# Row maxima of a unit turned by one transpose of 16 columns instead of four of 4, negated on 16 partitions, and sent as pieces of 128 tokens

## What is computed

```python
for lvl in range(LEVELS):                       # 4 levels
    x = query[:, ::2 ** lvl, :]
    outs.append(_mha(x, in_proj_w[lvl], in_proj_b[lvl], out_w[lvl], out_b[lvl]))
current = outs[-1]
for lvl in range(LEVELS - 2, -1, -1):
    current = _upsample_linear(current, outs[lvl].shape[1]) @ up_w[lvl].T + up_b[lvl] + outs[lvl]
...
h = silu(x @ w1 * s1) * (x @ w2 * s2)           # feed-forward part, widths 256 and 1024
h = gelu(gelu(h @ h1 * s) @ h2 * s);  y = h @ w3 * s3
```

## Time and profile before

| | before |
|---|---|
| median of 3 runs | 3819.87 us (3819.08 to 3824.79) |
| the profiled execution, its own time | 3822.95 us |
| its span in the trace | 3819.7 us |
| mean granted TensorE clock | 0.966 of full speed |
| PE busy | 3545.6 us, 93% |
| ACT busy | 2607.4 us, 68% |
| DVE busy | 2539.7 us, 66% |
| POOL busy | 1134.5 us, 30% |

### The profile page before, as it was taken

How to read it: one execution, slowest core, us unless ns; L and a number is a source line. 1 busy time by engine, 2 the same in 40 slices (tenths; PEclk the granted TensorE clock), 3 DMA queues, 4 the chain that set the end, 5 groups by cost and what they waited for, 6 DMA issues and landing times. The chain is left out here.

```text
span 3819.7 us, 59270 instructions
## 1 busy us (share of the span) xinstructions
PE 3545.6 (93%) x20995; PEld 1428.9 (37%) x20995; DVE 2539.7 (66%) x4805; ACT 2607.4 (68%) x3266; POOL 1134.5 (30%) x1060
## 2 busy tenths in 40 slices
PE   5899999989989999989989998859999999999998
PEld 3333333333333333333333332224444444444444
DVE  4787988988888888897897899833334333334333
ACT  2788788878878878878878888834444444444443
POOL 2243454454364364363354444220000000000000
PEclk6999989999999999999998999979999999999999
DMA  4523333332332342242342233110000000000000
GB/s 145 175 76 92 106 98 93 95 104 83 97 117 82 95 125 76 90 121 79 95 128 74 88 103 106 51 51 11 13 12 13 12 23 12 12 12 15 20 12 12
DMA packets 227902, 269.85 MB, mean 71 GB/s; under 512 B 51268, under 2 KB 187524, under 8 KB 226976
## 3 DMA queue, kind: packets, MB, share of 16 engines
q1 hardware_dynamic: 218352, 257.09, 22.6%
q10 hardware_dynamic: 9216, 8.39, 0.7%
HBM read 159.75 MB, written 101.45 MB: 68 GB/s over the span
## 5 line engine op out<-in xcount | busy, mean ns | idle before, releaser
L957 ACT ACTIVATE a_probs<-a_p_s,a_unit_now 128x1024 f32<-128x1024 f32 x1360 | 1442.4, 1109 | 300.7 <-PE a_p_s L1281 296.3
L1063 DVE TENSOR_REDUCE a_part_max<-a_p_r 128x1 f32<-128x512 f32 x2048 | 1304.1, 676 | 270.1 <-PE a_p_r L1294 265.8
L1294 PE MATMUL a_p_r<-a_k_st,a_q_st 48*128 48x512 f16 (+2 forms) x2944 | 912.2, 380 | 138.0 <-DVE a_part_max L1063 69.6
L1653 PE MATMUL p_h<-f_h_hi,f_w_hi 128*128 128x512 f16 x2048 | 776.3, 379 | 3.0 <-issue 3.0
L1653 PE MATMUL p_h<-f_h_lo,f_w_hi 128*128 128x512 f16 x2048 | 776.2, 379 | 0.0
L1311 PE MATMUL a_p_o<-a_probs,a_v_aug 128*17 128x512 f32 (+2 forms) x5888 | 739.0, 582 | 2.4 <-ACT a_raw L967 2.3
L1281 PE MATMUL a_p_s<-a_q_st,a_k_st 50*128 50x512 f16 (+2 forms) x2944 | 693.6, 374 | 30.7 <-ACT a_probs L957 30.6
L1294 PEld LDWEIGHTS a_p_r<-a_k_st,a_q_st 48*128 48x128 f16 x2944 | 222.7, 94 | 1164.4 <-DVE a_part_max L1063 799.2
L1515 ACT ACTIVATE f_h_f<-p_h,f_sc_now 128x512 f32<-128x512 f32 x256 | 176.0, 688 | 516.3 <-PE p_h L1653 514.3
L1063 DVE TENSOR_REDUCE a_row_max<-a_p_r 128x1 f32<-128x512 f32 (+2 forms) x672 | 426.2, 675 | 82.9 <-PE a_p_r L1294 81.2
L1462 POOL TENSOR_TENSOR f_rstd<-f_var_eps,f_minus_half 128x1 f32<-128x1 f32 x64 | 36.0, 563 | 1240.5 <-DVE f_var_eps L1608 1240.5
(11 more groups left out here) (157 smaller groups left out, 4616.2 us busy)
## 6 DMA issues: line engine op xcount, KB each, us to landing
qk_scratch<-a_qk_room SPq DMA_DIRECT2D x288, 128.0 KB
a_w_lo<-wqkv_inner SPq DMA_DIRECT2D x30, 768.0 KB, 4.5
a_a_lo<-a_attn SPq DMA_DIRECT2D x448, 32.0 KB, 2.0
a_q_st<-qk_scratch SPq DMA_DIRECT2D x64, 192.0 KB, 3.4
a_k_st<-qk_scratch SPq DMA_DIRECT2D x64, 192.0 KB, 4.4
a_o_lo<-wo_inner SPq DMA_DIRECT2D x24, 512.0 KB, 3.5
a_qk_room<-wf SPq DMA_DIRECT2D x23, 512.0 KB, 3.7
a_q_st<-qk_scratch SPq DMA_DIRECT2D x112, 96.0 KB, 2.2
```

Source lines behind the costliest of these rows:

```text
L957: act.activation(probs[:, s % 2, 2 * p:2 * p + 2, :], p_s[:, 2 * p:2 * p + 2, :], ACT.Exp, scale=unit_now[:, lvl:lvl + 1]).then_inc(exp_do ...
L1063: dve.reduce_max(out, src, AX.X).then_inc(max_read.sem, 1)
L1294: ins = pe.matmul(p_a[:, r * size:(r + 1) * size], q_st[rows_of(j, ROWS), query_at:query_at + 128], k_st[rows_of(j, ROWS), key_at:key_at + ...
L1653: ins = pe.matmul(out, a, c, start=first and n == 0, stop=last and n == len(terms) - 1)
```

## The change

`row_max` gets its last two axes swapped, so that the 16 maxima of a query (4 head groups by 4 blocks) lie in the order head, block. One transpose turns all 16 columns at once, into 16 partitions by 128 tokens, where before four transposes turned 4 columns each into 4 partitions by 512. ACT and POOL then work on 16 x 128 instead of 4 x 512. The DMAs send 8 partitions of 128 tokens each (256 bytes) where before they sent 2 of 512 (1024 bytes). So that these pieces form one row, the queries of a fine unit lie in `q_st` one behind the other; for that the "stack" of level 0 loads the queries of each unit of a pair by DMAs of its own: four for `q_st` where there were two, and the same bytes.

```diff
-        row_max = sb("row_max", [128, RING, NQ, HG])
-        neg_f = sb("neg_f", [HG, W])
-        neg_bf = sb("neg_bf", [HG, 2, 2, W], F16)
+        row_max = sb("row_max", [128, RING, HG, NQ])
+        neg_f = sb("neg_f", [HG * NQ, 128])
+        neg_bf = sb("neg_bf", [HG * NQ, 2, 2, 128], F16)
...
+        def query_spot(unit, j):
+
+            return unit.halves[unit.blk] * 2 * W + j % 2 * W
...
+                                    if t == 0 and lvl == 0:
+                                        for blk in range(2):
+                                            part = st[64 * row_half:64 * row_half + ROWS, at + blk * 2 * W:at + (blk + 1) * 2 * W].rearrange("p (h t) -> p h t", h=2)
+                                            sp.dma_start(part, src[:, :, blk * W:(blk + 1) * W]).then_inc(stacked[n].sem, 16)
+                                        continue
                                     sp.dma_start(dst, src).then_inc(stacked[n].sem, 16)
...
-                                    sp.dma_start(placed(q_st, slice(row_at, row_at + 1), UNITS[n], UNITS[n].blk),
-                                                 neg_bf[2 * row_half:2 * row_half + 2, n % 2, i, :]).then_inc(neg_placed[n % 2].sem, 16)
+                                    sp.dma_start(q_st[row_at:row_at + 1, query_spot(UNITS[n], 0):query_spot(UNITS[n], 0) + 2 * W].rearrange("p (r t) -> p r t", t=128),
+                                                 neg_bf[8 * row_half:8 * row_half + 8, n % 2, i, :]).then_inc(neg_placed[n % 2].sem, 16)
...
-                            act.activation(neg_f[:, :], p_a[0:HG, 0:W], ACT.Copy, scale=-1.0 / ONE).then_inc(neg_read.sem, 1)
+                            act.activation(neg_f[:, :], p_a[0:HG * NQ, 0:128], ACT.Copy, scale=-1.0 / ONE).then_inc(neg_read.sem, 1)
...
-                            for q in range(NQ):
-                                ins = pe.transpose(p_a[0:HG, q * 128:(q + 1) * 128], row_max[:, n % RING, q, :], ident[:, :])
-                            ins.then_inc(neg_mm.sem, 1)
+                            pe.transpose(p_a[0:HG * NQ, 0:128], row_max[:, n % RING, :, :].rearrange("p h q -> p (h q)"), ident[:, :])\
+                              .then_inc(neg_mm.sem, 1)
```

More of the change, by code:

```diff
@@ L495, in attention @@
         stored = [sig(f"stored{i}", SLOTS * sum(len(ps) for ps in PROJ[i::2]), 16) for i in range(2)]
-        stacked = [sig(f"stacked{n}", 4, 16) for n in range(len(STACKS))]
+        stacked = [sig(f"stacked{n}", 2 * (1 + len(us)), 16) for n, us in enumerate(STACKS)]
         v_mm, v_done = sig("v_mm", len(V_PAIRS)), sig("v_done", len(V_PAIRS))
@@ L1051, in steps @@
                                 neg_mm.wait(dve, it, u - 2)
-                            slot = row_max[:, u % RING, :, :].rearrange("p q h -> p (q h)")
+                            slot = row_max[:, u % RING, :, :].rearrange("p h q -> p (h q)")
                             q, j, kb, _ = maxima_of(u, m)[0]
                             if lvl == 0:
-                                out = part_max[:, u % RING, q * HG + j, kb:kb + 1]
+                                out = part_max[:, u % RING, j * NQ + q, kb:kb + 1]
                             elif lvl == 3:
-                                out = row_max[:, u % RING, q:q + 2, j:j + 2]
+                                out = row_max[:, u % RING, j:j + 2, q:q + 2].rearrange("p h q -> p q h")
                             else:
-                                out = slot[:, q * HG + j:q * HG + j + parts]
+                                out = row_max[:, u % RING, j:j + parts, q]
                             src = p_a.rearrange("p (r t) -> p r t", r=parts) if parts > 1 else p_a
@@ L1279, in steps @@
                                 for j in (p, p + 2):
-                                    key_at, query_at = spot(unit, half, j) + key, spot(unit, unit.blk, j) + i * size
+                                    key_at, query_at = spot(unit, half, j) + key, query_spot(unit, j) + i * size
                                     ins = pe.matmul(p_s[:, bank_of(j), i * size:(i + 1) * size], k_st[rows_of(j, ROWS + 2), key_at:key_at + 128],
@@ L1289, in steps @@
                             if m == 0 and u == STACKS[STACK_OF[u]][0]:
-                                stacked[STACK_OF[u]].wait(pe, it, 4)
+                                stacked[STACK_OF[u]].wait(pe, it, 2 * (1 + len(STACKS[STACK_OF[u]])))
                             for q, j, kb, r in maxima_of(u, m):
                                 key = q * 128 // size * size if parts > 1 else 0
-                                query_at, key_at = spot(unit, unit.blk, j) + q * 128, spot(unit, kb, j) + key
+                                query_at, key_at = query_spot(unit, j) + q * 128, spot(unit, kb, j) + key
                                 ins = pe.matmul(p_a[:, r * size:(r + 1) * size], q_st[rows_of(j, ROWS), query_at:query_at + 128],
```

## The result

| | before | after |
|---|---|---|
| median of 4 runs | 3820.23 us (3819.08 to 3824.79) | 3796.64 us (3794.89 to 3799.38) |
| span of the profiled execution | 3819.7 us | 3795.0 us |
| mean granted TensorE clock | 0.966 | 0.966 |

The ratio is 0.9937, with a 95% interval of 0.9919 to 0.9954: 23.6 us faster, or 0.6%. The forecast was 3798.

The account below looks back on a forecast made before the run. The attention stage is bound by a chain passing between PE, DVE and ACT, none of them full. PE 12.2, ACT 16.2 and POOL 1.5 sum to 29.9 us, three quarters taken as 22 us: 3798 us, range 3781 to 3813.

Parts of the forecast that it names:

- PE's term: Attention stage: three transposes fewer save 0.33 us a unit, 12.2 us over the 37 units on the chain.
- Which units of ACT: Middle batches: the chain passes ACT's pair in three units, the second and fourth of the batch and the third fine one.
- ACT's term: Attention stage: both ACT instructions at 128 elements save 0.65 us a unit, 16.2 us over 25 units on the chain.
- the factor of three quarters: Chosen share of the 29.9 us sum expected to be won, since the next chain is near: 22 us.
- POOL's term: POOL's subtraction falls from 1152 to about 415 ns, hidden except at two places on the chain: 1.5 us.
- The stack: 64 more issues on SP, 26 us of SP, hidden by the written order; at most 26 us if uncovered.
- DVE: Reductions to `row_max` write at another stride: at most 7 us of DVE, taken as 0.
- The rows' DMAs: Shorter pieces hardly end a score's wait more than once; smallest cover 1.5 us, at the fourth fine unit.
- waits of fine units for the rows: Sign that the forecast is wrong: scores at fine units wait for the DMAs of the rows.
- Absorbed: Rival: DVE's reductions of the maxima become the next wait; gain below 8 us, 3812 to 3827; chance 0.10.
- slower: Rival: rows land late and fine units' first scores wait; 42 us slower, 3862, from 6 us delay; chance 0.06.
- More than the chain: Rival: savings off today's chain count too, or transposes cost full duration; gain 30 to 50 us, 3770 to 3790; chance 0.22.

Follow-up runs that it names:

- e12: Changed kernel with both ACT instructions back at 512 elements, except at 128 in units 1, 3 and 9 of a batch: 3799.7 us, ratio 0.9942 to the kernel before.
- e0: The changed kernel itself, without any edit, timed again beside the kernel before: 3799.4 us, ratio 0.9940.
- e2: Changed kernel with both ACT instructions back at 512 elements, POOL and the single transpose kept: 3821.0 us, ratio 0.9995 to the kernel before.
- e5: Changed kernel with four transposes and POOL at 512 elements, so only ACT's instructions are short: 3801.2 us, ratio 0.9943 to the kernel before.
- e1: Changed kernel with its one transpose done four times into the same place: 3799.4 us, ratio 0.9940 to the kernel before.
- e4: Changed kernel with ACT and POOL back at 512 elements, single transpose and new way of the rows kept: 3821.0 us, ratio 0.9998 to the kernel before.
- e10: Changed kernel with its one transpose done eight times into the same place: 3820.1 us, ratio 0.9990 to the kernel before.
- e3: Kernel before with only the new layout of the queries and its 64 further DMA issues: 3823.4 us, ratio 1.0001 to the kernel before.
- e7: Changed kernel with SP's "neg" task 0.6 steps sooner in the order: 3798.2 us, ratio 0.9938 to the kernel before.
- e8: Changed kernel with only the first ACT instruction, `neg_f`, back at 512 elements: 3804.3 us, ratio 0.9953 to the kernel before.
- e9: Changed kernel with only the second ACT instruction, `neg_bf`, back at 512 elements: 3804.4 us, ratio 0.9957 to the kernel before.
- e11: Changed kernel with the second ACT instruction, the upper float16 piece, done by POOL instead: 3796.8 us, ratio 0.9935 to the kernel before.

## Why the prediction was right, and where it was right by luck

**The total** came out as forecast, 23.6 us against 22, and lies in the range. That it fits so well is luck: PE's term of 9 us was nearly all wrong, ACT's of 12 us was a little small, and the clock, which the forecast didn't have, made up for most of the rest. What was right is the cause: only what lies on the chain counts, and ACT's pair lies on it at three units of a batch.

**Which units of ACT** (forecast: in a middle batch the second and fourth unit and the third fine one). Right. e12 shortens only these and has the time of e0 within 0.3 us, by runs of two chips, and in the traces the same mean batch (300.41 and 300.44 us). Beside them 58-59 answers with 0.15 us a batch.

**ACT's term** (16.2 us, 12 after the factor of three quarters). The columns 84-4, 34-35, 78-79 and 58-59 give 0.65 + 0.65 + 0.44 + 0.15 = 1.89 us a batch, between before and e0. Over the whole run that is some 14 us: the border and 78-79 come seven times, and in the last batch 34-35 gives 0.21 and 74-75 gives 0.60. The forecast had paid the full 0.65 at units 1 and 3, which lead into `raw`, and 0.5 at unit 9, ahead of exponentials. It was the full 0.65 at units 3 and 9, and 0.44 at unit 1. The measured worth of the short instructions as a whole, 21.6 us (e2 against e0) and 21.7 (e5 against before), is 7 to 8 us more; 3 to 6 of these the traces show at the clock's step (below).

**PE's term** (12.2 us, 9 after the factor). Wrong: e1 and e4 measure nothing, and the steps show 0.17 us a batch, 1.2 us in all, at one place. The step that failed is the count of 37 units on the chain. Walking backwards, the forecast went on to the transposes wherever PE had run without an idle gap. Where DVE's reduction had released the next bank only just before PE got to it, as in the rows of e0 and e1 above, the way through DVE was as long, and a faster PE only waited. That this is so at each of the other units of the 37 is not shown one by one, but the idle time of PE behind the transposes grew by 0.20 us a unit over all 120, and the total says the same. The price was right (0.60 us for four, 0.28 for one); by e10 the cover is real but thin, since four further transposes cost 20.7 us. The rule of the Trainium skill, page "TensorE: Matmul & The Clock Gate", section "Part 4: PE-mode transpose", some 275 ns in a kernel, is the duration that the rows have (286 ns); as a cost it would have been wrong by more, since three transposes added 0.32 us to PE's work and none to the time.

**POOL's term** (1.5 us). e5 against e1 is 1.9 us, or 1.3 with each taken against the kernel before on its own chip; it fits and doesn't show it. **The stack** (nothing, since 4.5 to 11 steps hide it): e3, 1.0001. **DVE** (nothing): its busy time is the same.

**The rows' DMAs** (hardly more than one wait). Seven scores waited, 6.2 us by the list of waits. At six of them it was only the weight load, at the first score of a batch, and the steps there are as long in e7, where nothing waits: a wait listed is not time lost. The seventh was at the fourth fine unit, where the forecast saw 1.5 us of cover. That cover was gone in one batch of eight, and the step was 1.5 us longer in e0 and 0.8 in the first profiled execution. By its own words, waits of fine units for the rows were a sign against the forecast; it came true at one unit of 64 and is too small to be seen in the times.

**The rivals.** "Absorbed" and "slower" did not come. "More than the chain" was wrong in its mechanism, since units outside the chain brought 0.15 us a batch. What the forecast didn't have is the clock: 4-5 is 0.64 us a batch shorter in e0 than before, 0.92 in e1, 4 to 6 us over the middle batches. With it the sum nearly closes: 14 + 1.2 + 4 to 6 is 19 to 21. The two profiled executions of before and e0 are 18.8 us apart, before and after 24.7, and the medians 23.0 to 23.6, so 2 to 5 us of the medians have no place in it. The first batch, which the table leaves out, differs by several us from trace to trace in no order that follows the edits. It also goes far to explain the odd result of e8 and e9: each has half of ACT's gain missing (0.33 + 0.33 + 0.13 = 0.79 us a batch, some 6 us by the steps and 4 to 5 by the times) and all of the clock's kept; e2 misses both.

**What stays open**: why the clock falls at step 4 in 18 of 24 batches where both ACT instructions are long in all units, and in 9 of the other 60. Longer ACT work ahead of the place goes with it, but e12, with long pairs in all but three units, has 1 of 6, the two batches of e0 above have the same rows just before the place and come out differently, and e11, with the least ACT work, has 3 of 6. A rival that no run tests is that the fall depends on when the place comes, as the batches with both long also take 3 us longer (303 against 300); e10 speaks against the length alone, with 302.7 us and no fall. No run here changed the clock alone, so its share is read from the traces, each of one execution, and is not isolated by an experiment.

## What to carry to other kernels

A chain that is walked back by "what was busy before" overcounts an engine that arrives just as another releases it; before such work is put on the chain, look how late the releaser of the next instruction was, and take the later of the two ways. Where a saving is taken in halves and the halves don't add up, compare the time of each step between traces rather than the total: steps that answer evenly are the chain, steps that jump between two values are something else, here the clock. The mean granted clock (0.966 before and after) hides it; a window around the step shows it.

## What the runs showed of the hardware

- At the same place of one execution, with the same busy time of PE ahead of it (1.05 of 2.00 us), sixteen products of 256 columns took 1.06 us at a granted clock of 1.00 and 1.91 us at 0.50. The Trainium skill, page "TensorE: Matmul & The Clock Gate", section "A second HAM failure mode: psum-queue depth-cycling", says that small idle times between groups of products that cycle through banks can make the clock go back and forth. The trace fits this and doesn't show it: the products ahead had waited 0.32 and 0.54 us for a bank, but they had waited just as long at the place that kept its clock.
- ACT's copy of 512 elements takes 571 ns with 4 partitions and with 16 (e12). POOL's time goes by the elements of a partition too: 1152 ns for 512 elements with 4 partitions, 1151 with 16 (e4), and 418 for 128 elements with 16.
- A DMA between places of SBUF in 8 pieces of 256 bytes has a median issue of 632 ns where 2 pieces of 1024 bytes had 560. The Trainium skill, page "DMA: Bandwidth & Descriptors", section "Specifications", has 512 B as the least for full rate. At 2 KB a DMA no run here shows a cost of it in the kernel's time: e4, with the short pieces and ACT and POOL at 512, takes as long as the kernel before (0.9998).
